# Self attention on one core: even and odd heads in two halves of the array's rows, PSUM banks dealt three, four and one

## The reference

```python
def attn(x, Wq, bq, Wk, bk, Wv, bv, Wo, bo, W_cross, shift_weights, gate):
    Q, K, V = heads(x @ Wq.T + bq), heads(x @ Wk.T + bk), heads(x @ Wv.T + bv)
    scores = (gt * scores_cross + (1.0 - gt) * scores_conv) * scale   # both bilinear in Q and K
    scores = where(causal, scores, -inf)
    return softmax(scores) @ V @ Wo.T + bo
x = x + attn(layernorm(x), ...)
x = x + cross_attention(layernorm(x), ctx, mask)
x = x + (silu(h @ w_gate.T) * (h @ w_up.T)) @ w_down.T            # h = layernorm(x)
```

## Time and profile before

| | |
|---|---|
| median of three runs (lowest, highest) | 1246.96 us (1246.66, 1250.59) |
| profiled execution, its span (the page gives no other time for it) | 1246.4 us |
| PE busy in it | 1081.7 us, 87% |
| DVE, ACT, POOL busy | 792.2, 557.3, 216.0 us |
| mean granted TensorE clock | 0.935 of full |

### The profile page before, as it was taken

One profiled execution on the slowest core, in us unless ns is written; L12 is line 12 of the kernel. 1 busy time (PEld: TensorE's weight loads), 2 busy tenths in 40 slices (PEclk: granted clock), 3 DMA queues, 4 the chain that ended last, 5 costly groups with the idle time before them and its releaser, 6 DMA issues. The chain is left out here.

```text
span 1246.4 us, 23540 instructions
## 1 busy us (share of the span) xinstructions
PE 1081.7 (87%) x7116; PEld 640.1 (51%) x7164; DVE 792.2 (64%) x1705; ACT 557.3 (45%) x1022; POOL 216.0 (17%) x175
## 2 busy tenths in 40 slices
PE   1888969998999899999998665769999689999997
PEld 1677424443444344444443443434444278888886
DVE  4799837776777777777781775745555255555452
ACT  2456126665666666666666111216666321111110
POOL 4155510000000000000001233310000133333321
PEclk9899769998999989999999777859999889999999
DMA  6389892443344434444022578885666422222200
GB/s 196 104 289 309 252 149 70 85 91 71 75 86 87 87 69 86 86 87 90 18 74 87 170 218 234 245 235 148 173 177 163 148 68 68 68 67 67 67 18 34
DMA packets 132838, 153.30 MB, mean 123 GB/s; under 512 B 29003, under 2 KB 104319, under 8 KB 132735
## 3 DMA queue, kind: packets, MB, share of 16 engines
q1 hardware_dynamic: 126207, 145.74, 45.5%
q10 hardware_dynamic: 6528, 6.29, 1.5%
HBM read 87.69 MB, written 64.95 MB: 122 GB/s over the span
## 5 line engine op out<-in xcount | busy, mean ns | idle before, releaser
L687 DVE TENSOR_REDUCE self_pm<-bank 128x1 f32<-128x512 f32 (+3 forms) x608 | 365.4, 656 | 100.0 <-PE bank L772 68.7
L738 ACT ACTIVATE self_prob<-bank 128x512 f32<-128x512 f32 (+1 forms) x608 | 325.6, 577 | 184.1 <-PE bank L794 110.1
L786 PE MATMUL bank<-self_stq,self_stk 98*128 98x512 bf16 (+3 forms) x768 | 225.7, 334 | 24.9 <-DMA self_stq<-self_mrow 11.8
L763 PE MATMUL bank<-self_stk,self_stq 96*128 96x512 bf16 (+3 forms) x768 | 228.7, 342 | 8.1 <-DVE self_mrow L684 5.4
L806 PE MATMUL bank<-self_prob,self_va 128*32 128x512 f32 (+3 forms) x1536 | 163.7, 507 | 4.3
L763 PEld LDWEIGHTS bank<-self_stk,self_stq 96*128 96x128 bf16 x768 | 71.2, 100 | 162.4 <-DVE self_pm L687 111.8
L961 POOL TENSOR_TENSOR rin<-rin,bo_b 128x1024 f32<-128x1024 f32 x8 | 26.1, 3259 | 538.1 <-DMA min_<-mask_BxSxS_bk 538.1
L1768 ACT ACTIVATE e_sg<-bank 128x512 f32<-128x512 f32 x48 | 28.7, 599 | 191.9 <-PE bank L184 191.9
L786 PEld LDWEIGHTS bank<-self_stq,self_stk 98*128 98x128 bf16 x768 | 70.1, 99 | 83.8 <-issue 32.0
L738 ACT ACTIVATE cross_prob<-bank 96x512 f32<-96x512 f32 x128 | 74.8, 593 | 63.2 <-PE bank L791 63.0
L687 DVE TENSOR_REDUCE cross_pm<-bank 128x4 f32<-128x384 f32 x128 | 70.0, 557 | 35.0 <-PE bank L768 33.2
(11 more groups left out here) (189 smaller groups left out, 1423.9 us busy)
## 6 DMA issues: line engine op xcount, KB each, us to landing
qk<-a_parts SPq DMA_DIRECT2D x32, 384.0 KB, 4.8
self_stq<-qk SPq DMA_DIRECT2D x192, 64.0 KB, 2.9
self_stk<-qk SPq DMA_DIRECT2D x96, 128.0 KB, 5.2
cross_stq<-xqs SPq DMA_DIRECT2D x32, 384.0 KB, 4.7
vs<-a_vst SPq DMA_DIRECT2D x8, 1024.0 KB, 5.5
self_va<-vs SPq DMA_DIRECT2D x16, 512.0 KB, 7.0
od<-self_u SPq DMA_DIRECT2D x16, 512.0 KB, 2.7
oin<-od SPq DMA_DIRECT2D x32, 256.0 KB
```

The source lines that it names most:

```text
L687: nc.vector.tensor_reduce(pm[:, k, h0:h0 + hb, r], src[:, 0:hb * w].rearrange("p (h w) -> p h w", h=hb), AX, ALU.max).then_inc(s_mxe, 1)
L738: nc.scalar.activation(ops.prob[:, u % NPS, 0:hb * n], bank[ST_BANKS[u % 3]][0:KP, 0:hb * n], ACT.Exp).then_inc(s_ex, 1)
L763: mm = nc.tensor.matmul(dst[:, h * w:(h + 1) * w], stq[i][0:R, half, h0 + h, r * P:(r + 1) * P], stk[i][0:R, h0 + h, k0:k0 + w], start=(h ...
L786: mm = nc.tensor.matmul(dst[0:KP, h * n:(h + 1) * n], stk[i][0:RM, h0 + h, kt * KP:(kt + 1) * KP], stq[i][0:RM, half, h0 + h, q0:q0 + n], ...
```

## The change

Self attention gets a function of its own, `self_attention`. Q and K are cut into two fp32r parts (three products, 3 x 16 = 48 rows), even heads lie in rows 0 to 63 of the array, odd heads in rows 64 to 127, two heads of each parity side by side. Units come in pairs, one unit per parity, in two banks. The diagonal is added by matmuls of 64 rows too, with two constants `pick` and `off` that POOL makes in stage 1. Banks: three for maxima, four for scores, one for sums of values (before 3, 3, 2). Values lie with 17 columns for each head in place of 32. Every hardware loop is replaced by unrolled code.

```diff
+SELF_BANKS = (0, 1, 2), (3, 4, 5, 6), (7, 7)
+Q_CUTS = ((0, 0, 1), (1, 0, 2))
+K_CUTS = ((0, 0, 2), (2, 0, 1))
-        def sweep(eng, chunk, peeled=1):
-            with eng.Fori(0, B - peeled) as b:
-                chunk(b, 0, True)
-                chunk(b, 1, True)
-            for b in range(B - peeled, B):
+        def sweep(chunk):
+            for b in range(B):
                 chunk(b, 0, True)
                 chunk(b, 1, b < B - 1)
...
@@ stage 1, POOL, between power1(g, 0, 0) and power1(g, 0, 1)
+                def step(ins):
+                    ins.then_inc(s_pk, 1)
+                    made[0] += 1
+                    g.wait_ge(s_pk, made[0])
...
+                nc.gpsimd.tensor_copy(pick[:], pickf[:])
+                for i in range(2):
+                    nc.gpsimd.tensor_copy(off[:, :, i], offf[:, :, 0])
...
@@ self_attention: the units
+            for half in range(2):
+                for r in range(4):
+                    if half:
+                        mx_pairs += [(half, 1, r, ((hh,), (hh,)), 0, 512, False) for hh in range(2)]
+                    w = (r + 1) * P
+                    hhs = [(0, 1)] if w <= 256 else [(0,), (1,)]
+                    mx_pairs += [(half, 2 * half, r, (hh, hh), half * 512, w, True) for hh in hhs]
...
+                for kt in range(4 * half + 4):
+                    diag = kt >= 4 * half
+                    q0 = (kt % 4) * P if diag else 0
+                    n = 512 - q0
+                    hhs = [(0, 1)] if n <= 256 else [(0,), (1,)]
+                    st_pairs += [(half, kt, hh, q0, n, diag) for hh in hhs]
...
+            LAG = 2
+            LATE = 2
+            for p in range(NSP):
+                plan.append(("s", p, 0))
+                if p == LATE:
+                    plan.append(("r", (NMX - 1,), 0))
+                upto = max(0, p - LATE + 1) * len(items) // (NSP - LATE)
+                plan += [("r", n, 1) for n in items[at:upto]]
+                at = upto
+                plan += [("p", s, 0) for s, x in enumerate(sets) if x[3] - 1 == p - LAG]
+                plan += [("p", s, -1) for s, x in enumerate(sets) if x[3] - 1 == NSP + p - LAG]
...
@@ self_attention, tensor: a pair of maxima units (scores are made alike, with stk and stq exchanged)
+                    t.wait_ge(s_mxe, g * NMX + ns[-1] + 1)
+                    for j in range(len(hs[0])):
+                        for par in range(2):
+                            rows = slice(64 * par, 64 * par + ML)
+                            mm = nc.tensor.matmul(dst[par][:, j * w:(j + 1) * w],
+                                                  stq[i][rows, hs[par][j], (4 * half + r) * P:(4 * half + r + 1) * P],
+                                                  stk[i][rows, hs[par][j], k0:k0 + w], ...)
+                    for c in range(2):
+                        for par in range(2):
+                            rows = slice(64 * par, 64 * par + 64)
+                            k1 = w - P + c * P // 2
+                            mm = nc.tensor.matmul(dst[par]...[:, :, k1:k1 + P // 2],
+                                pick[rows, 0, c], off[rows, 0, 0:len(hs[0])], start=False, stop=(c == 1), ...)
...
+                def products(g, s):
+                    if fresh:
+                        t.wait_ge(s_u, 2 * g + half + (1 if PVB[0] != PVB[1] else 2))
...
@@ self_attention, sync
+                for g in range(G):
+                    maxima(g, 1)
+                    if g:
+                        store(g - 1)
+                    if g + GB - 1 < G:
+                        sp.wait_ge(s_pv, NPS + g * NST)
+                        load_group(sp, ops, (g + GB - 1) // GB, (g + GB - 1) % GB)
+                    if g + 1 < G:
+                        maxima(g + 1, 0)
...
@@ self_attention, gpsimd: all of rows 32 to 63 of each half, before the loads
+                        for par in range(2):
+                            nc.gpsimd.memset(stk[i][64 * par + 32:64 * par + 64].bitcast(F32), -1.0).then_inc(s_set, 1)
...
@@ load_self: four DMAs for Q, four for K
+            for par in range(2):
+                for slot, part, number in Q_CUTS:
+                    sp.dma_start(stq[64 * par + HD * slot:64 * par + HD * (slot + number)].bitcast(F32),
+                                 heads[0][par, HD * part:HD * (part + number)]).then_inc(ld, 16)
...
@@ stage 2
+                        self_placed(sp, 1)
                         load_group(sp, self_ops, 0, 0)
...
                 barrier(sp, 2)
+                self_placed(sp, GB)
                 load_group(sp, self_ops, 0, 1)
                 self_sync(sp, True)
                 load_group(sp, self_ops, 0, 2)
...
-                def low(b, u, n):
-                def middle(b, u, n):
-                    nc.vector.scalar_tensor_tensor(rest[:, n], bank[QKB[n]][:], qkb[:, n // 2, n % 2:n % 2 + 1],
-                                                   parts[:, u, n, 0], ALU.add, ALU.subtract).then_inc(s_r, 1)
+                    nc.vector.scalar_tensor_tensor(parts[:, u, n, 1], bank[QKB[n]][:], qkb[:, n // 2, n % 2:n % 2 + 1],
+                                                   parts[:, u, n, 0].bitcast(F32), ALU.add, ALU.subtract).then_inc(s_r, 1)
```

More of the change, by code:

```diff
@@ new lines, in _ @@
+                step(nc.gpsimd.memset(offf[:], 0.0))
+                for which, spare in ((0, halfp - 1), (1, 0)):
+                    for c in range(2):
+                        for half in range(2):
+                            where(pickf[:, which, c, c * halfp:(c + 1) * halfp], ALU.not_equal, 1.0,
+                                  -half * halfp, [[-1, halfp]], 1)
+                        at = c * halfp + spare
+                        step(nc.gpsimd.memset(pickf[:, which, c, at:at + 1], 0.0))
+                    c = 1 - which
+                    for half in range(2):
+                        where(pickf[:, which, c, (1 - c) * halfp:(2 - c) * halfp], ALU.not_equal, 1.0,
+                              -half * halfp - spare, [[0, halfp]], 1)
+                    sign = 1 - 2 * which
+                    for half in range(2):
+                        where(offf[:, which, half], ALU.is_ge, NEG, -sign * half * halfp, [[-sign, halfp]], sign)
+                    if which:
+                        where(offf[:, 1, 0], ALU.is_ge, 0.0, halfp - 1, [[0, halfp]], -1)
+                    else:
+                        where(offf[:, 0, 1], ALU.is_ge, 0.0, -halfp, [[0, halfp]], 1)
+                    step(nc.gpsimd.tensor_tensor(offf[:, which, 0], offf[:, which, 0], offf[:, which, 1], ALU.add))
+                    for half in range(2):
+                        where(offf[:, which, 0], ALU.not_equal, NEG, -half * halfp - spare, [[0, halfp]], 1)
@@ L618, in attention, with steps @@
             stq, stk, va, mk, ld, NLD = ops.stq, ops.stk, ops.va, ops.mk, ops.ld, ops.n_loads
-            def steps(eng, step):
-                with eng.Fori(0, B - 1) as b:
-                    for i in range(GB):
-                        step(b, i, GB)
-                for i in range(GB):
-                    step(B - 1, i, GB - 1 - i)
+            def steps(step):
+                for g in range(G):
+                    step(g // GB, g % GB, min(GB, G - 1 - g))
             def after(b, i, n):
@@ L660, in step @@
                                  ops.u[:, i % 2]).then_inc(us[i % 2], 16)
-                steps(sp, step)
+                steps(step)
                 barrier(sp, stage)
@@ L718, in vector @@
                     return
-                steps(v, step)
+                steps(step)
                 following.early_vector(v)
@@ L742, in step @@
                     outputs(b, i, 1)
-                steps(a, step)
+                steps(step)
                 barrier(a, stage)
@@ L830, in tensor @@
                 t.wait_ge(s_set, GB)
-                steps(t, step)
+                steps(step)
                 barrier(t, stage)
@@ L874, in place, with __init__ @@
                         self.mk.append(sb(f"{self.name}mk{i}", [SK, S], BF16))
+        class SelfOperands:
+            def __init__(self, load_qk, n_qk, v_src):
+                self.stq, self.stk, self.va = [], [], []
+                self.load_qk, self.v_src, self.m_src = load_qk, v_src, None
+                self.ld = [sem(f"self_ld{i}") for i in range(GB)]
+                self.n_loads = n_qk + 1
+            def place(self, n):
+                for i in range(len(self.stq), len(self.stq) + n):
+                    self.stq.append(sb(f"self_stq{i}", [P, HG // 2, S], F32R))
+                    self.stk.append(sb(f"self_stk{i}", [P, HG // 2, S], F32R))
+                    self.va.append(sb(f"self_va{i}", [P, S // P, HD + 1, HG]))
         def load_group(sp, ops, b, i):
@@ L1245, in _ @@
                 turn(0, 0)
-                sweep(t, chunk)
+                sweep(chunk)
                 t.wait_ge(s_xt, 2 + 2 * NCH)
@@ L1498, in _ @@
                 turned(0, 0)
-                sweep(a, chunk)
```

(5 more changed lines are left out.)

377 lines of the change are left out of this document (296 added, 81 removed).

## The result

The changed kernel takes 1404.38 us (three runs, 1396.91 to 1404.62) where the kernel before takes 1246.96: 12.3% slower, ratio 1.1231 [1.1188, 1.1275]. Forecast were 1183 us and a range up to 1228. The page first, part 1 and three lines of part 5; the latter read: line, engine, operation, count, then busy time and mean ns of one, then the engine's idle time just before them and what ended most of it.

The account below looks back on a forecast made before the run. PE was taken to bound self attention, DVE next. Group 0's store at 200 us plus 14 x 28.2 gave 595, the last group 24 more, 619 for 682.8: 64 us saved, 1183 us, range 1138 to 1228.

Parts of the forecast that it names:

- the step on banks: Self attention, three banks for pairs: a pair waits for two free banks; stall up to 0.25 us a set of products.
- The upper end: Upper end of a self-attention group's period: 11.2 + 27.9 - 8.5 = 30.6, with 0.4, 31 us.
- Rival (b): Self attention: the banks decide, each set of products stalls DVE; period 30.5 us, total 1216 us; chance 0.14.
- Rival (c): Self attention: PE's clock falls once in each group, 3.8 us; period 32 us, total 1238 us; chance 0.07.
- PE's work: PE's busy time in a self-attention group after the change: 25.1 us, ends 21.3 and 27.9.
- Rival (d): Self attention: the array's halves don't run together; 34 us a group with waits, total 1271 us; chance 0.13.
- DVE: DVE's work in a self-attention group, with 40 units for 38: 24.3 us, up from 24.05.
- The period that is left: Time of one self-attention group, from DVE-paced slots, PE-paced slots and 0.4 us for sums of values: 28.2 us.
- Loops: Unrolling removes two loop turns in self attention, 14 us; straight code costs nothing there, other stages gain 0.
- Stage 2: PE's wait for DVE's normalising goes; barrier 3 us earlier (148.8 to 146), ends 8 earlier and 2 later.
- Entry: Behind the barrier: memsets 10.8 us offset by a shorter DMA queue; first scores about 166, store of group 0 at 200.
- Opening: Stage 1: POOL's 29 small steps and three copies, 12 us, fit in a 17.7 us gap; cost 0.

Follow-up runs that it names:

- banks431: The changed kernel with four banks for maxima, three for scores, one for sums of values: 1280.1 us, ratio 1.0253.
- after_even: all431_even with the banks dealt 3, 4, 1 again, as in the changed kernel: 1341.1 us, ratio 1.072.
- all431_even: Changed kernel with banks 4, 3, 1, Q/K stores' rows at one distance, maxima's DMAs before loads, more maxima pairs in slots without products: 1213.4 us.
- half_reduce: The changed kernel, banks 3, 4, 1, with DVE reducing half of each unit's columns and exponentials scaled by 0.01: 1280.6 us, ratio 1.0269.
- double_max: The changed kernel with each pair of maxima matmuls issued twice into the same bank: 1466.6 us, ratio 1.1746.

## Why the prediction was wrong

**The period of a group failed, in the step on banks.** That step read "a pair waits for two free banks, DVE then has one unit of 0.6 us as cover", and put the stall at up to 0.25 us a set of products, "in the upper end". The upper end's own sum, 11.2 + 27.9 - 8.5 + 0.4 = 31, has no term for it, so it was priced at nothing. The cover was right and its use was wrong in three ways. The stall stands ahead of pairs of maxima, at every second one about, and is longer (PE's loads waited for DVE 131 times for 90.3 us between 280 and 800, 0.69 us each and some 7 a group). What must fit under 0.6 us is a pair until its result can be read, 0.50 us at full clock and 0.80 at half, with 0.2 of hand-over, and not the 0.24 to the next start. And scores and products queue behind the waiting pair, so ACT starves too. Rival (b) named the mechanism, with a period of 30.5; it was 37.5 in most groups and 39.5 on the mean, as the clock fell with it. banks431 and after_even beside all431_even show that the deal of the banks is worth 124 to 128 us, and half_reduce that it is DVE's hold on a bank that counts, with 124 us too.

**The clock failed as a rival of its own.** Rival (c) had one fall a group for 3.8 us. Measured is a mean of 0.82 over a regular group, with some 14 us at half clock in two falls, and 0.54 to 0.78 over the five long ones. I had weighed it as independent of (b), "against: PE has 2.1 of 2.8 us to do even in DVE's slots". The stall and the clock came together: double_max shows that added work doesn't lift the clock, half_reduce that a shorter stall does. Both should have been one rival, on the slower side. What the clock itself answers to stays open.

**PE's work held roughly.** 25.1 us forecast, ends 21.3 and 27.9; 26.6 to 27.1 busy in windows at full clock. Of the missing 1.5 to 2 us some 1.2 lie in the pairs, by my estimate: 0.24 each was right behind another pair (0.22), but behind a set of products it is 0.34, and a group has twelve sets. Rival (d) is out. Where the page TensorE: Matmul & The Clock Gate of the Trainium skill lets a load last columns divided by 1.2 GHz (section on LDWEIGHTS), an estimate by that rule is 0.107 us for the 128 columns of a load and 0.21 for the two loads of a pair. A pair behind a pair takes 0.22 in all, which agrees, and can't tell the loads from the pass beside them. Two of the sums were off by little: 18,432 x 0.235/512 is 8.5 and not 8.4, and 96 loads at 0.107 us are 10.2 and not 10.3. DVE held: 24.3 forecast, 24.5 in banks431; ACT 21.5 and 20.8.

**The period that is left, 28.2 forecast.** Its ends were 25 to 31 where they were worked out and 26 to 30 where the range was made from them. It came out at 30.46 with the better deal and 29.04 with the even plan. PE's extra 1.5 to 2 us is one part. The other I had for two engines, DVE and PE; the hand-over between PE and ACT, with three banks for scores or with slots of 0.7 and 1.7 us in turn, was not in the sum.

**Loops held.** 14 us forecast, 12 measured alone, and straight code kept 31.1 us a group.

**Stage 2 failed, in the step on bytes.** I counted engine waits and bytes (3.0 to 3.15 MB a chunk) and took the barrier 3 us earlier. The engines did as forecast, a chunk took 9.4 us at first, but of the stores I costed the bytes alone, not their form: eight heads of 16 rows each, two cuts interleaved. They held SP for 14.5 us a chunk, and the barrier came 36.5 us later. Mended, it came at 142.9, inside my ends. Rows of before could bound it only from one side: there such an issue of 384 KB, with another order of rows, took SP 0.37 us (median between 60 and 130), four of them 7.4 us with the waits between (its timeline at 67.98). That SP could be held by its issues was left out.

**Entry.** Memsets (11.06 us for 10.8), issues (0.45) and the four small DMAs (2.70 for 2) held. What failed was group 0 itself, 55.6 us from its first scores to its store where I had 34 (200 - 166) and before has 42.4, from the bank step again (40.8 in banks431), and the landing, 7 us for about 3, with nine large loads ahead of the four small ones and nine more right behind. **Opening**: no cost, as forecast.

Put together: the deal of the banks 124 us, the stores 33, SP's order 12 behind the mended stores (alone 7, not clear of noise), the plan 22. With all of them mended the change is worth 1247 - 1213 = 34 us, of which 12 are the loops; my 64 were too many for that too. Some 9 of the missing 30 are the last group, forecast at 24 us, measured at 23.3 with the change's deal and 32.8 with the better one.

## What to carry to other kernels

When work is issued in pairs, count buffers in pairs: an odd ring of three lets the next pair start only when the first of the last two has been read, so a round is producer plus one consumer, one after the other. Check it with the producer's time to a readable result, at the lower clock too, since in this kernel the stall and the clock's fall came together. When a store's shape changes, cost the queue that issues it by the shape and not by its bytes, and compare the DMA share with the bandwidth: a middling share with an issuer that is never idle (0.59 here) points at the shape.

## What the runs showed of the hardware

- The same 256 KB of 2 KB rows cost SP 1.31 us an issue as eight heads of 16 rows with a gap and 0.52 as 128 rows at one distance (medians between 60 and 130 us); the core's DMA went from 207 to 334 GB/s (73 to 83).
- Two fp32r matmuls in the two halves of the array's rows take the time of one: 0.22 us for 512 columns each, loads included, behind another pair.
- The granted clock stays at half in the 24 us of the first maxima with PE busy for 54% of them with three banks, and with 72% in banks431 too (window 166 to 182):

```profile
166.00:182.00 16.00, 11.52 (x55) 5.20 (x55) 15.70 (x31) 0.00 (x0) 0.00 (x0) 0.50 0.63 218
```

- Issuing each pair of maxima twice (double_max) did not bring it back. What makes it rise in the middle of a group (near 643 us) and fall near 660 stays open.
